# A graph layer with routed experts: the one-hot products of the tile stage read their weights as fp32, through a small copy

## The chip, the cores and the metric

One Trainium2 chip, one of its cores. The metric is the device time of one execution, in microseconds. The kernel before takes 3982.83 us, the median of three runs (3973.16 to 3984.31).

## What is computed

The reference, cut to what matters:

```python
def _L0_gnn_ref(x, W, bias, edge_row, edge_col, edge_val):   # x: layer-normalised, 12500 x 256
    h = x @ W
    msgs = h[edge_col] * edge_val[:, None]                   # 212500 edges
    agg = jax.ops.segment_sum(msgs, edge_row, num_segments=12500)
    return agg + bias

x = x + _L0_gnn_ref(_layernorm(x), W, bias, src, dst, edge_weight)
x = x + _L0_ffn_ref(_layernorm(x))      # 8 experts 256 -> 512 -> 256, the best two per row by a router
```

A row of `h` is fetched for every edge, weighted by `edge_weight` and added to the row of the node `src`. The expert part works on the result, row by row.

## The kernel before

The rows are cut into `NT` = 98 tiles of `P` = 128 nodes. The kernel has three parts.

**Preparation** (up to about 910 us). The edges are counted and sorted by node tile. The sorted list goes to DRAM as units. A unit is 128 partitions of `RUN` = 8 edges: 1024 edges, of which each has the row number of `h` to fetch, the node number and the weight as two fp16 halves, high and low. `h` is written to DRAM as `h_table`, each row as a high and a low fp16 half of 256.

**The tile stage** (about 910 to 3350 us), to which the change belongs. Tiles follow each other, and each engine has its own program, ordered by semaphores:

- SyncE, `serve` (lines 671 to 677): for each unit it waits until TensorE has used up the unit four before (`s_summed`), makes room for GpSimd (`s_room`) and loads a later unit of the list into the ring `listed` (`RL` = 8 slots).
- GpSimd, `gather` (lines 790 to 801): per unit eight indirect transfers (line 798), each of 128 rows of `h_table`, into the ring `stage` (`RU` = 4 units). It says that a unit is there (`s_gath`) in the middle of the next one.
- VectorE, `target_rows` (lines 1386 to 1407), once for each pair of a unit and a tile that the unit touches. This is called a pass here. Line 1392 subtracts the tile's first node number (`rel`). Line 1395 compares it with 0 to 127 (`equal`, one-hot rows of 8 x 128). Line 1403 multiplies the one-hot with the weights, once for the high halves and once for the low halves, each 128x1024, into the ring `target` (`TR` = 8 passes). There are 326 passes: a unit that lies across the border of two tiles has two.
- TensorE, `chunks` (lines 1821 to 1838): per pass eight times two matmuls, `target` by `stage` (lines 1832 and 1834), summed in PSUM. Line 1837 closes the tile.
- VectorE, `epilogue` (lines 1448 to 1464): from line 1458 on it adds the sum to `x`, normalises twice at once (lines 1426 to 1446) and writes `zb` (line 1446). TensorE turns `zb` (line 1851), ScalarE copies it, and the router's logits follow (lines 1856, 1858).
- Between these runs the dense expert work on half of the tiles: `hidden` (line 1885), ScalarE's GELU, the split into halves by VectorE (line 1510, an fp32 minus an fp16 operand), `expert` (line 1902) and the sums (line 1528). The rows of the other tiles are routed and handled in the last part.

What sets the order around the change is VectorE's own program, `step(t)`: the rest of tile t's passes (seldom any), the passes of tile t + 1 (`ahead`), then the epilogue of tile t, then the expert work and the choice of experts. TensorE's is `chunks(t)`, `hidden`, `transposes(t)` (which waits for `zb`), `expert`, `logits(t)`. So the passes of tile t + 1 stand on VectorE ahead of the epilogue of tile t.

**The routed part** (from about 3381 us). GpSimd scatters the routed rows by expert (line 815), TensorE works through blocks of 256 rows (lines 1954, 1970, 1987), and GpSimd gathers the results (line 830).

Of the kernel before, what the change touches and what calls it, by code (L numbers as in the profile page):

```python
# [5 lines left out]
def gnn_moe_layer_kernel(  # L6
# [42 lines left out]
    fp32 = mybir.dt.float32  # L49
# [6 lines left out]
    ds = bass.ds  # L56
    AX = mybir.AxisListType

    P = 128
    N, D = x.shape  # L60
    E = src.shape[0]
    NE, _, HID = W1.shape
    KD = D // P
    KH = HID // P
# [13 lines left out]
    RUN = 8  # L78
# [43 lines left out]
    with ctx:  # L122
        ctx.enter_context(nc.allow_non_contiguous_dma(reason="small constants, one element per row"))

        def sb(name, shape, dt):
            return ctx.enter_context(nc.sbuf_tensor(name, shape, dt))

        def sem(name):
            return ctx.enter_context(nc.semaphore(name))
# [88 lines left out]
        wfull = sb("wfull", [P, 2, SB, 32], fp32)  # L218
        wT = sb("wT", [P, P], fp32)
        rel = sb("rel", [P, RUN], fp16)  # L220


        UNIT = RUN * 2 * D
# [233 lines left out]
        s_gat = [sem(f"s_gat{k}") for k in range(RU)]  # L457
        s_gath = sem("s_gath")
        s_rel = sem("s_rel")
        s_eq = sem("s_eq")  # L460
        s_tgt = sem("s_tgt")
        s_summed = sem("s_summed")
# [59 lines left out]
        def reached(eng, s, value, gate=True):  # L522

            if isinstance(value, int):
                if value > 0:
                    eng.wait_ge(s, value)
                return
            eng.wait_ge(s, value)
            if gate:
                eng.sem_inc(s_gate, 1)  # L530
# [549 lines left out]
        def _(dve):  # L1080
# [305 lines left out]
            def target_rows(u, t):  # L1386
                i = u + t
                at = (u % RL) * WORDS
                listed_f = listed[:, :, :].rearrange("p u w -> p (u w)")
                listed_h = listed_f.bitcast(fp16)  # L1390
                reached(dve, s_list, 16 * (u + 1), gate=False)
                nc.vector.tensor_scalar(rel[:, :], listed_f[:, ds(at + RUN, RUN)], tile_no[:, ds(t, 1)], None,  # L1392
                                        ALU.subtract).then_inc(s_rel, 1)
                reached(dve, s_rel, i + 1, gate=False)
                nc.vector.tensor_tensor(  # L1395
                    equal[:, :, :, :], pair_no[:, :, :].unsqueeze(1).to_broadcast([P, RUN // 2, P, 2]),
                    rel[:, :].rearrange("p (j e) -> p j e", e=2).unsqueeze(2).to_broadcast([P, RUN // 2, P, 2]),
                    ALU.is_equal).then_inc(s_eq, 1)
                reached(dve, s_eq, i + 1, gate=False)
                reached(dve, s_summed, i + 1, gate=False)  # L1400
                for part in range(2):
                    two = listed_h[:, ds(2 * at + (4 + part) * RUN, RUN)].rearrange("p (j e) -> p j e", e=2)
                    made = nc.vector.tensor_tensor(  # L1403
                        target[:, ds((i % TR) * TGT + part * (TGT // 2), TGT // 2)].rearrange(
                            "p (j s e) -> p j s e", j=RUN // 2, e=2),
                        equal[:, :, :, :], two.unsqueeze(2).to_broadcast([P, RUN // 2, P, 2]), ALU.mult)
                made.then_inc(s_tgt, 1)

            def table(t, b, least, biggest):
                return dve.value_load(t[0:1, ds(b, 1)], min_val=least, max_val=biggest)  # L1410

            def ahead(t):
                first = table(lo_i, t, 0, NU)
                end = table(ahead_i, t, 1, NU + 1)
                with dve.Fori(first, end) as u:
                    target_rows(u, t)

            def rest(t):
                first = table(ahead_i, t, 1, NU + 1)
                end = table(end_i, t, 1, NU + 1)  # L1420
                with dve.If(first < end):
                    with dve.Fori(first, end) as u:
                        target_rows(u, t)
# [217 lines left out]
            nc.vector.memset(acc[:, 0, :, :].rearrange("p q d -> p (q d)"), 0.0)  # L1641
            nc.vector.memset(xTh[:, 0, :, :].rearrange("p k n -> p (k n)"), 0.0)
            nc.vector.memset(xTl[:, 0, :, :].rearrange("p k n -> p (k n)"), 0.0).then_inc(s_clear, 1)
            ahead(0)
            for t in range(NT + SB + 1):
                step(t)
# [62 lines left out]
        def _(pe):  # L1709
# [111 lines left out]
            def chunks(b):  # L1821
                reached(pe, s_x1, b, gate=False)
                nc.tensor.matmul(psA[:, :], one_h[:, :], bias_hl[:, :], start=True, stop=False)
                first = pe.value_load(lo_i[0:1, ds(b, 1)], min_val=0, max_val=NU)
                end = pe.value_load(end_i[0:1, ds(b, 1)], min_val=1, max_val=NU + 1)
                with pe.Fori(first, end) as u:
                    i = u + b
                    reached(pe, s_gath, u + 1, gate=False)
                    reached(pe, s_tgt, i + 1, gate=False)
                    for c in range(RUN):  # L1830
                        at, rows = (i % TR) * TGT + (c // 2) * (2 * P) + c % 2, (u % RU) * UNIT + c * (2 * D)
                        nc.tensor.matmul(psA[:, :], target[:, ds(at, P, 2)], stage[:, ds(rows, 2 * D)], start=False,  # L1832
                                         stop=False)
                        last = nc.tensor.matmul(psA[:, 0:D], target[:, ds(at + TGT // 2, P, 2)],  # L1834
                                                stage[:, ds(rows, D)], start=False, stop=False)
                    last.then_inc(s_summed, 1)
                nc.tensor.matmul(psA[:, 0:1], zero_h[:, 0:P], zero_h[:, 0:1], start=False,
                                 stop=True).then_inc(s_agg, 1)
# [88 lines left out]
            for t in range(NT + SB + 1):  # L1927
                i = t - SB
                if t < NT:
                    chunks(t)  # L1930
                if t - 1 in place_of:
                    ranks(t - 1)
                if 0 <= i < NEX and i % NE == 0:
                    weights_T(i // NE)
                if 0 <= i < NEX:
                    hidden(i)
                if t < NT:
                    transposes(t)
                if 1 <= i <= NEX:
                    expert(i - 1)  # L1940
                if 0 <= i < NEX and i % NE == 0:
                    b2_terms(i // NE)
                if t < NT:
                    logits(t)
# [50 lines left out]
            for n in range(NBL):  # L1995
                h, m = block_of(n)
                e = pe.value_load(expert_i[0:1, h, m:m + 1], min_val=0, max_val=NE - 1)
# [39 lines left out]
```

## Time and profile before

| | |
|---|---|
| median of three runs | 3982.83 us (3973.16 to 3984.31) |
| the profiled execution | 3981.84 us, of it the span of the profile 3979.7 us |
| mean granted TensorE clock | 0.919 of full speed |
| tile stage | first sum closed at 936.7 us, last at 3344.9 us |
| busy share PE, DVE, ACT, POOL | 80%, 61%, 33%, 64% |

PE is TensorE's matmul side, DVE is VectorE, ACT is ScalarE, POOL is GpSimd, SP is SyncE. All times count from the start of the span, in us. In a line of the timeline stand start, duration, engine, line of the kernel, operation and the tensors (out <- in); in square brackets stands how long the engine had been idle and what ended that. "x2" says that two like instructions are merged, and the duration is that of both together. In a group of instructions stand the shape and the count, then the busy time in us and the mean of one in ns, then the idle time before them. "issue" is time in which the engine waited for nothing that the profile shows.

### The profile page before, as it was taken

The numbers are of one execution on the slowest core, as the hardware profiler recorded it, in microseconds if no ns is written. First come the engines' busy times: TensorE is split into PE (matmuls) and PEld (weight loads), VectorE is DVE, ScalarE is ACT, GpSimd is POOL, SyncE is SP. The second block draws the span as 40 slices with busy tenths as digits, with TensorE's granted clock in tenths as the row PEclk, the third lists the DMA queues.
The fourth block names the chain that finished last, engine by engine and source line by source line (L and its number), as shares of the span: only waits on it lengthen the run. The fifth ranks groups of instructions, "written<-read, shape, count | busy, mean of one in ns | idle before, by whom it ended". The sixth has DMA issues, their size and how long they took to land.

```text
span 3979.7 us, 75949 instructions
## 1 busy us (share of the span) xinstructions
PE 3194.3 (80%) x20888; PEld 2076.7 (52%) x20888; DVE 2415.8 (61%) x6037; ACT 1331.0 (33%) x2857; POOL 2538.3 (64%) x2491
## 2 busy tenths in 40 slices
PE   6677767824788899898988998998988989099983
PEld 4444444412455555555555555555555556088862
DVE  9699334514666666666666666676666665144563
ACT  1354656720222222222222222222222222066651
POOL 1241457877777777777777777777777776630264
PEclk9899989966899999999999999999999999599996
DMA  4341110003434334434343434343334346552463
GB/s 154 106 117 60 33 36 15 8 12 92 117 110 119 110 113 114 119 112 120 112 117 110 117 110 120 109 115 108 114 111 120 108 118 104 175 165 86 125 202 113
DMA packets 288427, 420.20 MB, mean 106 GB/s; under 512 B 89733, under 2 KB 218314, under 8 KB 288138
## 3 DMA queue, kind: packets, MB, share of 16 engines
q0 software_dynamic: 109280, 279.33, 25.2%
q1 hardware_dynamic: 112536, 72.81, 6.4%
q10 hardware_dynamic: 66324, 64.42, 5.1%
q8 instruction: 157, 2.57, 0.3%
q14 instruction: 130, 1.06, 0.1%
HBM read 339.36 MB, written 76.98 MB: 105 GB/s over the span
## 4 chain that ended last, share of the span: by engine, by line
PE 36%; DVE 14%; issue 11%; POOL 7%; DVEq 5%; DMA 2%; ACT 1%; SPq 1%; ACTq 0%; POOLq 0%
PE twin L1902 7%; PE twin L1832 6%; PE bank L1902 6%; POOL area L798 5%; DVE area L1395 3%; PE twin L1834 3%; DVEq L1410 2%; DVE area L1403 2%; PE twin L1885 2%; PE bank L1885 2%; PE twin L1970 2%; PE twin L1987 2%; POOL zs L815 2%; PE bank L1970 1%; PE bank L1987 1%
## 5 line engine op out<-in xcount | busy, mean ns | idle before, releaser
L798 POOL DMA_INDIRECT area<-h_table,listed x1856 | 1864.3, 1004 | 606.0 <-issue 542.9
L1832 PE MATMUL twin<-area 128*128 x2608 | 880.9, 385 | 76.7 <-POOLq L797 38.3
L1834 PE MATMUL twin<-area 128*128 x2608 | 718.2, 275 | 0.0
L973 ACT ACTIVATE area<-twin,b_t 128x512 f32<-128x512 f32 x192 | 132.0, 687 | 1446.0 <-PE twin L1885 860.2
L1403 DVE TENSOR_TENSOR area<-area,listed 128x1024 f16 x652 | 422.6, 689 | 106.9 <-DVE area L1395 94.9
L1832 PEld LDWEIGHTS twin<-area 128*128 x2608 | 257.0, 99 | 415.2 <-issue 183.3
L766 POOL DMA_INDIRECT edge_list<-area,didx x256 | 313.0, 1223 | 77.1 <-issue 77.1
L1902 PE MATMUL twin<-w2h,area 128*128 128x256 f16 x1536 | 338.6, 317 | 0.0
L751 POOL TENSOR_TENSOR area<-area 128x256 f16<-128x256 f32 x98 | 80.9, 829 | 339.8 <-ACT area L862 339.6
L1834 PEld LDWEIGHTS twin<-area 128*128 x2608 | 257.1, 99 | 49.1 <-issue 0.2
L1902 PE MATMUL bank<-w2h,area 128*128 128x256 f16 x1536 | 267.7, 273 | 0.0
L1785 PE MATMUL twin<-area 128*128 128x512 f16 (+1 forms) x448 | 173.0, 392 | 113.7 <-ACT area L909 65.9
L1392 DVE TENSOR_SCALAR rel<-listed,tile_no 128x8 f16 x326 | 77.8, 239 | 297.9 <-issue 251.0
L1510 DVE TENSOR_TENSOR area<-area 128x512 f16<-128x512 f32 x384 | 244.0, 688 | 17.2 <-ACT area L975 17.2
L1902 PE MATMUL twin<-w2l,area 128*128 128x256 f16 x768 | 243.7, 317 | 0.0
L1395 DVE TENSOR_TENSOR area<-pair_no,rel 128x1024 f16<-128x1024 f16 x326 | 225.7, 692 | 11.2
L917 ACT ACTIVATE area<-twin 128x512 f16<-128x512 f32 (+1 forms) x448 | 228.9, 565 | 5.5 <-PE twin L1785 5.2
L1885 PE MATMUL twin<-area,w1h 128*128 128x512 f16 x768 | 229.5, 380 | 0.0
L1885 PE MATMUL bank<-area,w1h 128*128 128x512 f16 x768 | 228.8, 380 | 0.0
L1851 PE MATMUL bank<-ident,zb 128*128 128x128 f32 x196 | 44.9, 316 | 207.7 <-DVE zb L1446 207.4
L1671 DVE TENSOR_TENSOR area<-area 128x512 f16<-128x512 f32 x132 | 91.4, 692 | 197.8 <-ACT area L1045 197.8
L828 POOL DMA_DIRECT2D area<-out_dram x50 | 29.3, 586 | 285.5 <-issue 220.6
(339 smaller groups left out, 6505.3 us busy)
## 6 DMA issues: line engine op xcount, KB each, us to landing
area<-h_table,listed POOLq DMA_INDIRECT x1856
area<-in_x_dram SPq DMA_DIRECT2D x194, 128.0 KB, 2.2
area<-zs SPq DMA_DIRECT2D x66, 256.0 KB, 2.9
ys<-area ACTq DMA_DIRECT2D x66, 256.0 KB
out_dram<-area ACTq DMA_DIRECT2D x100, 128.0 KB, 2.6
h_table<-area SPq DMA_DIRECT2D x97, 128.0 KB, 1.7
xt<-in_x_dram ACTq DMA_DIRECT2D x97, 128.0 KB
area<-in_L_ffn_W_dram ACTq DMA_DIRECT2D x16, 512.0 KB, 4.0
```

The costliest lines, as they stand in the source:

```text
L766: pool.indirect_dma_start(out=list_v, out_offset=bass.IndirectOffsetOnAxis(ap=didx[B % 4][:, j, r:r + 1], axis=0), in_=record[:, B % 4, j, ...
L798: pool.indirect_dma_start(out=stage[:, (k % RU) * UNIT + 2 * D * c:(k % RU) * UNIT + 2 * D * (c + 1)], out_offset=None, in_=h_table[:, :], ...
L917: nc.scalar.activation(ohs[:, g % 2, PER * j:PER * j + w, :].rearrange("p c s -> p (c s)"), slot(n)[:, 0:w * P], ACT.Exp, scale=SHARP).the ...
L973: nc.scalar.activation(h32[:, m, :], psH[m][:, :], ACT.Gelu, scale=1.0 / WSCALE, bias=b1_t[:, e * KH + m:e * KH + m + 1])
L1395: nc.vector.tensor_tensor(equal[:, :, :, :], pair_no[:, :, :].unsqueeze(1).to_broadcast([P, RUN // 2, P, 2]), rel[:, :].rearrange("p (j e) ...
L1403: made = nc.vector.tensor_tensor(target[:, ds((i % TR) * TGT + part * (TGT // 2), TGT // 2)].rearrange("p (j s e) -> p j s e", j=RUN // 2, ...
L1510: nc.vector.tensor_tensor(hl[:, i % 2, m, :], h32[:, m, :], hh[:, i % 2, m, :], ALU.subtract).then_inc(s_hl, 1)
L1785: nc.tensor.matmul(slot(n)[:, 0:w * P], digits_T[:, g % 2, :], rh[:, PER * j:PER * j + w, :].rearrange("p c s -> p (c s)"), start=True, st ...
L1832: nc.tensor.matmul(psA[:, :], target[:, ds(at, P, 2)], stage[:, ds(rows, 2 * D)], start=False, stop=False)
L1834: last = nc.tensor.matmul(psA[:, 0:D], target[:, ds(at + TGT // 2, P, 2)], stage[:, ds(rows, D)], start=False, stop=False)
L1885: last = nc.tensor.matmul(psH[m][:, :], a, r, start=(k == 0 and n == 0), stop=(k == KD - 1 and n == 2))
L1902: last = nc.tensor.matmul(half_bank(q), a, r[:, e, m, :], start=(m == 0 and n == 0), stop=(m == KH - 1 and n == 2))
```

## The change

The weights of a pass, two times eight fp16 values per partition, are copied into a new fp32 tile `share`, and the two products of line 1403 read their weights from there. The one-hot operand and the result stay fp16. Before the copy overwrites `share` it waits until the products of the pass before are done (`s_tgt`); for that the semaphore starts at 1, and TensorE waits for one more.

```diff
@@ -218,6 +218,7 @@
         rel = sb("rel", [P, RUN], fp16)
+        share = sb("share", [P, 2, RUN], fp32)
@@ -457,6 +458,7 @@
         s_rel = sem("s_rel")
+        s_share = sem("s_share")
@@ -1391,15 +1393,19 @@
                 nc.vector.tensor_scalar(rel[:, :], listed_f[:, ds(at + RUN, RUN)], tile_no[:, ds(t, 1)], None,
                                         ALU.subtract).then_inc(s_rel, 1)
+                reached(dve, s_tgt, i + 1, gate=False)
+                nc.vector.tensor_copy(share[:, :, :].rearrange("p f c -> p (f c)"),
+                                      listed_h[:, ds(2 * at + 4 * RUN, 2 * RUN)]).then_inc(s_share, 1)
                 reached(dve, s_rel, i + 1, gate=False)
                 nc.vector.tensor_tensor(
                     equal[:, :, :, :], pair_no[:, :, :].unsqueeze(1).to_broadcast([P, RUN // 2, P, 2]),
                     rel[:, :].rearrange("p (j e) -> p j e", e=2).unsqueeze(2).to_broadcast([P, RUN // 2, P, 2]),
                     ALU.is_equal).then_inc(s_eq, 1)
+                reached(dve, s_share, i + 1, gate=False)
                 reached(dve, s_eq, i + 1, gate=False)
                 reached(dve, s_summed, i + 1, gate=False)
                 for part in range(2):
-                    two = listed_h[:, ds(2 * at + (4 + part) * RUN, RUN)].rearrange("p (j e) -> p j e", e=2)
+                    two = share[:, part, :].rearrange("p (j e) -> p j e", e=2)
                     made = nc.vector.tensor_tensor(
...
@@ -1641,6 +1647,7 @@
+            dve.sem_inc(s_tgt, 1)
             ahead(0)
@@ -1826,7 +1833,7 @@
-                    reached(pe, s_tgt, i + 1, gate=False)
+                    reached(pe, s_tgt, i + 2, gate=False)
```

## Rows read from the trace of the kernel before

**Rows 1.** The page: busy shares, the chain that ended last, the group of line 1832.

```profile
PE 3194.3 (80%) x20888; PEld 2076.7 (52%) x20888; DVE 2415.8 (61%) x6037; ACT 1331.0 (33%) x2857; POOL 2538.3 (64%) x2491
...
PE 36%; DVE 14%; issue 11%; POOL 7%; DVEq 5%; DMA 2%; ACT 1%; SPq 1%; ACTq 0%; POOLq 0%
...
L1832 PE MATMUL twin<-area 128*128 x2608 | 880.9, 385 | 76.7 <-POOLq L797 38.3
```

**Rows 2.** Line 1837 alone: ns min/median/max, first and last start.

```profile
L1837 PE MATMUL twin<-zero_h x98: 172/172/173, 936.7 to 3344.9; 1*128 1x1 f16 x98
```

**Rows 3.** PE's waits, 1300 to 3300: us in total, times, longest.

```profile
PE bank L1851 <- DVE zb L1446: 166.7, 54, 5.7
...
PE twin L1832 <- POOLq L797: 0.3, 1, 0.3
```

**Rows 4.** Timeline of DVE in one tile (four passes, then the epilogue).

```profile
2092.43 0.23 DVE L1392 TENSOR_SCALAR rel<-listed,tile_no 128x8 f16 x1 [3.25 <-issue]
...
2097.49 0.23 DVE L1392 TENSOR_SCALAR rel<-listed,tile_no 128x8 f16 x1
2097.75 0.69 DVE L1395 TENSOR_TENSOR area<-pair_no,rel 128x1024 f16<-128x1024 f16 x1
2098.77 1.29 DVE L1403 TENSOR_TENSOR area<-area,listed 128x1024 f16 x2 [0.33 <-DVE area L1395]
2099.98 0.22 DVE L1392 TENSOR_SCALAR rel<-listed,tile_no 128x8 f16 x1
...
2102.54 0.41 DVE L1458 TENSOR_TENSOR area<-xt,twin 128x256 f32<-128x256 f32 x1
...
2105.90 0.41 DVE L1446 TENSOR_SCALAR zb<-area,mv,rs 128x256 f32<-128x256 f32 x1
```

**Rows 5.** Timeline of PE in the same tile.

```profile
2101.55 0.38 PE L1885 MATMUL bank<-area,w1l 128*128 128x512 f16 x1
2106.46 0.41 PE L1851 MATMUL bank<-ident,zb 128*128 128x128 f32 x2 [4.53 <-DVE zb L1446]
```

**Rows 6.** Timeline of DVE and PE in the next tile.

```profile
2130.40 0.41 DVE L1446 TENSOR_SCALAR zb<-area,mv,rs 128x256 f32<-128x256 f32 x1
...
2131.91 0.38 PE L1851 MATMUL bank<-ident,zb 128*128 128x128 f32 x2
```

**Rows 7.** Groups of DVE by shape, whole span: line 1403.

```profile
L1403 DVE TENSOR_TENSOR area<-area,listed 128x1024 f16 x652 | 422.6, 689 | 106.9 <-DVE area L1395 94.9 <-PE twin L1834 12.0
```

**Rows 8.** The same view: subtractions of fp16 from fp32, and a small operation.

```profile
L1510 DVE TENSOR_TENSOR area<-area 128x512 f16<-128x512 f32 x384 | 244.0, 688 | 17.2 <-ACT area L975 17.2
...
L1469 DVE TENSOR_TENSOR area<-xT,area 128x256 f16<-128x256 f32 x48 | 20.0, 416 | 9.5 <-ACT area L962 9.5
...
L1542 DVE TENSOR_TENSOR eqr<-iota,ixrf 128x16 f32<-128x16 f32 x50 | 8.8, 176 | 1.7
...
L1659 DVE TENSOR_TENSOR area<-area 1x2048 f16<-1x2048 f32 x1 | 2.3, 2281 | 0.0
```

**Rows 9.** The chain, 2000 to 2120, and busy times of 2101.7 to 2111.5.

```profile
2081.49 2.62 PE twin L1902 x24
...
2106.87 4.29 PE twin L1902 x24
...
2101.70:2111.50 9.80, 5.27 (x33) 3.94 (x32) 7.37 (x25) 2.31 (x5) 7.56 (x8) 0.83 0.50 143
```

The last of these rows has the window and its length, then the busy time and count of PE, PEld, DVE, ACT and POOL, then the granted clock, the DMA share and GB/s.

**Rows 10.** Timeline of POOL at the end of the stage.

```profile
3372.56 0.95 POOL L798 DMA_INDIRECT area<-h_table,listed  x1 [0.30 <-issue]
3381.39 1.00 POOL L815 DMA_INDIRECT zs<-area,slot_i  x1 [7.88 <-DMA area<-h_table,listed]
```

**Rows 11.** Line 798: group of 1300 to 3300, all durations, one gather.

```profile
L798 POOL DMA_INDIRECT area<-h_table,listed x1506 | 1513.2, 1005 | 488.8 <-issue 441.1 <-SPq L675 39.2 <-DMA listed<-edge_list 5.2
...
L798 POOL DMA_INDIRECT area<-h_table,listed x1856: 947/953/1492, 907.9 to 3372.6; - x186
...
2003.42 1.45 POOL L798 DMA_INDIRECT area<-h_table,listed  x1 [0.31 <-issue]
```

## The prediction, made before the changed kernel was run

> **What bounds the kernel now.** I read the page first [rows 1]: VectorE (DVE) is busy 61% of the span, TensorE (PE) 80%, GpSimd (POOL) 64%. No engine is full, so the averages decide nothing. The chain of waits is shared by PE (36%), DVE (14%) and time at issue (11%). The change lies in one stage only, the loop over 98 node tiles. By its last matmul of each tile it paces at (3344.9 - 936.7) / 97 = 24.83 us per tile [rows 2].
>
> Next, who waits for whom in that stage. Between 1300 and 3300 us, some 80 tiles, PE waits 166.7 us in 54 waits for zb, the normalised tile that DVE's line 1446 writes [rows 3]. It waits 0.3 us for gathers, and the products of line 1403, which the change edits, are no large waits of their own. What PE lacks is not the products but what DVE does behind them.
>
> The timeline of one tile shows why [rows 4]. DVE runs the passes for the next tile's units (compare, two products) first, and only then the epilogue of this tile. In the tile shown it makes four passes from 2092.43, the epilogue starts at 2102.54, right behind the last product, and zb is finished at 2106.31. PE had finished its own work at 2101.93 and stood still until 2106.46 [rows 5]. In this tile every microsecond in a pass is a microsecond of the tile. The other kind: in the next tile PE had four iterations and DVE three passes; zb was finished at 2130.81 and PE came to it at 2131.91 without a wait [rows 6]. There DVE has about 1.1 us to spare.
>
> The 652 products of line 1403 [rows 7] are two a pass, so 326 passes over 98 tiles, 3.33 per tile, so one tile in three has a fourth pass. Of the 80 tiles 26 do not wait (32 of 98). The 54 waits average 3.1 us; where the pass count of DVE is four they are 4 to 4.5, as here, so the rest are near 2: about a third of the tiles each.
>
> **The price of one pass.** A pass now takes 2.49 us from one line 1392 to the next (2097.49 to 2099.98, [rows 4]).
>
> The products. The instruction of 128x1024 with all operands fp16 takes 0.689 us [rows 7]. After the change one operand is fp32. The rows nearest to that are the mixed subtractions, fp32 minus fp16 into fp16: 0.416 us for 256 elements, 0.688 for 512, and 2.281 for 2048 on one partition [rows 8]. 512 mixed elements cost what 1024 of fp16 do. Between the last two an element costs (2281 - 688) / 1536 = 1.037 ns, so 1024 take 0.688 + 0.531 = 1.22 us. The other pair gives 1.063 ns and 1.23 us. What these rows do not show is the operand that repeats eight values, so the lower bound is no change, 0.69 us; the upper is 1.23. I take 1.22: +0.53 for each of two, +1.06 a pass.
>
> The copy of 16 elements is new. The nearest row is an operation of 128x16 at 0.176 us [rows 8]. It stands between line 1392 and the comparison, where 0.03 us was free. Its wait for s_tgt asks for the last product of the pass before, which ends 0.08 us after line 1392 starts (2098.77 + 1.29 against 2099.98); behind it in DVE's queue stand the copy and the comparison. Two things pull the price apart: the address of the copy may be worked out only after that wait, and the 0.33 us between comparison and product [rows 4] may get shorter, since the products no longer work out an address in listed. Bounds: -0.10 us (the gap shrinks and the copy hides) to +0.33 (0.18 of copy and 0.15 of address work). I take +0.11, the middle. The later wait for s_share is on something long finished: nothing. The other edits, the pre-increment and PE's wait for i + 2, only shift a count by one: nothing. So a pass grows by 1.17 us, with ends at 0.96 and 1.39 as long as the product slows.
>
> **The sum, against the profiled execution (3981.84 us; the median of the three runs is 3982.83, 1 us away).**
> - 321 passes (all but the first tile's five, which lie under the first gathers) by 1.17: +376.
> - The 32 tiles in which DVE was early give 1.1 us of cover each: -35.
> - The first tiles wait for gathers: 38.3 us of PE's idle time at line 1832 are put to POOL over the whole span [rows 1] and 0.3 in the window of [rows 3]. POOL runs on meanwhile; I count half as given back: -18.
> - TensorE's clock. After the wait of 4.53 us the first 24 products of line 1902 took 4.29 us, against 2.62 in the tile before, where the wait was short [rows 9]; the granted clock of that stretch was 0.83, so part of it was at 1.2 GHz and not 2.4. That is 1.67 us. The third of tiles that now waits about 2 us will wait about 5.5 and pays it: 32 by 1.67 = +53. The third with no wait will wait about 2.4, between the two cases; half of them: +27. The last third pays already.
> - The end of the stage. Now POOL's last gather starts at 3372.56, 28 us after PE's last sum, and the scatter that the next stage waits for starts at 3381.39 [rows 10]. With slower tiles POOL is a full ring of four units ahead and ends soon after PE. The scatter then moves up by 15 to 20 us relative to the stage: -18.
>
> Sum: 376 - 35 - 18 + 53 + 27 - 18 = +385, so 3981.84 + 385 = 4367 us. The stage would go from 24.8 to about 28.9 us per tile. DVE's new busy time (652 by 0.53, and 326 copies) is +400 us, so almost none of it is hidden.
>
> What late DVE leaves others waiting for: PE for zb; ACT behind PE; the ring of targets (eight deep) stays ahead, for the passes of a tile are still made a tile early.
>
> **GpSimd.** A gather takes 0.953 us and 0.30 between, mean 1.005 [rows 11]: 1856 / 98 = 18.9 per tile by 1.305 is 24.7 us, as long as a tile now. It waits for room 39 us in 2000 [rows 11], so it is nearly the bound itself. At 28.9 us per tile it has 4 us to spare. But gathers get longer under DVE's two-input operations: 1.45 us at 2003.42 [rows 11], while DVE ran four of the mixed subtractions. The trace puts all such lengthening at 0.05 us on the mean gather, 1 us per tile; products 1.8 times as long make that 1.5 to 2, within the slack, so nothing is added.
>
> The Trainium skill (SBUF — State Buffer, Who interferes with whom) speaks more strongly against the change: a Vector instruction with two SBUF inputs locks out a GpSimd instruction that reads SBUF until it ends. By that rule each gather that meets a product would wait some 0.6 us on average, about 6 per tile, and POOL would need 28 us: still just under the tile, and the sum would stand. The trace agrees on the direction alone; its median gather is 0.953 us.
>
> **The rivals.**
> - Not slower: the product keeps its rate. The mechanism lies in line 1403: if the repeated fp32 operand costs no reading of its own, the product stays at 0.69 us, the copy fills the gap and one address less is worked out. Then a pass changes by -0.10 to +0.33 us; near zero the time is 3980, at the far end 4090. It decides at a product under 0.72 us. Against it: every mixed row runs at the slow rate. 0.04, most of it no change.
> - Hidden: GpSimd paces the stage, and DVE's time disappears under 24.7 us per tile. For it: the gathers fill the stage. Against it: PE waits 166.7 us for zb and 0.3 for gathers, and a tile cannot end before its DVE passes do. 3985 us. 0.02.
> - The clock goes further down. Waits of 5.5 to 9 us may cost twice 1.67 us in every tile: 97 by 1.67 = +160, 4527 us. For it: the longest waits now are 5.7 us [rows 3], so nothing longer is shown. 0.09.
> - GpSimd becomes the bound after all. If every gather that meets a product waits the whole of it (6 by 1.2), POOL needs 24.7 + 7.2 = 32 us per tile: (32 - 24.8) by 97 = +700, 4680 us. Against it: the median gather. 0.04.
> - The forecast: 0.81.
>
> **How the numbers follow.** The likeliest case gives 4367. Its bounds: a pass at +0.96 gives 308 in place of 376, and no clock loss takes off another 53 to 80, but hardly both: 4270. A pass at +1.39 gives +70, and with some more clock loss 4490, which takes in a part of the third rival. About 0.2 is left out. About 0.3% (12 us) is what a measurement of this kernel can tell from no change. Faster 0.01, same 0.04, slower 0.95.
>
> **What would show it.** In the profile after: line 1403 at 1.22 us x652 (under 0.72: the first rival); 3.6 to 3.7 us from one line 1392 to the next; PE's waits for zb at 5 to 6 us on the mean and in nearly every tile; 24 products at 4.3 us in most tiles, and a granted clock near 0.9 in the stage; GpSimd waiting for room 3 to 4 us per tile where it now waits half a microsecond; the last gather close behind PE's last sum; the stages before and after unchanged. The prediction is wrong if a pass grows by 1.2 us and the tile by much less (something hides it), or if PE waits for gathers at line 1832.

## The result, and the profile after

The changed kernel takes 4363.06 us, the median of four runs (4358.88 to 4364.65), against 3983.57 us for the kernel before beside it. The ratio is 1.0957, with a 95% interval of 1.0937 to 1.0977: 380 us slower. The forecast was 4367 us, 1.096 of the kernel before.

The page of the changed kernel (a line of the kernel has a number higher by 2 to 7 than before: 1392 is now 1394, 1403 is 1409, 1446 is 1452, 1832 is 1839, 1851 is 1858, 1902 is 1909, 798 is 800):

```profile
span 4359.8 us, 76276 instructions
PE 3263.3 (75%) x20888; PEld 2110.6 (48%) x20888; DVE 2786.0 (64%) x6363; ACT 1333.9 (31%) x2857; POOL 2717.3 (62%) x2491
```

DVE's busy time is up by 370 us (400 were forecast), and its share only from 61% to 64%, since the span grew as much. A reader of shares alone would not see that DVE's work sets the pace.

Its groups by shape, whole span, against [rows 7] and the 128x16 of [rows 8]:

```profile
L1409 DVE TENSOR_TENSOR area<-area,share 128x1024 f16 x652 | 776.9, 1232 | 97.9 <-issue 83.3 <-DVE area L1400 9.2 <-PE twin L1841 5.4
...
L1397 DVE CAST share<-listed 128x16 f32 x326 | 59.2, 181 | 5.6 <-issue 0.4
```

The product went from 0.689 to 1.232 us, the rate of the mixed subtractions. The copy takes 0.181 us.

The end of one pass, two whole passes and what follows them in the timeline of DVE, against [rows 4]:

```profile
2191.80 1.21 DVE L1409 TENSOR_TENSOR area<-area,share 128x1024 f16 x1
2192.93 0.22 DVE L1394 TENSOR_SCALAR rel<-listed,tile_no 128x8 f16 x1
2193.18 0.17 DVE L1397 CAST share<-listed 128x16 f32 x1
2193.26 0.69 DVE L1400 TENSOR_TENSOR area<-pair_no,rel 128x1024 f16<-128x1024 f16 x1
2194.23 2.43 DVE L1409 TENSOR_TENSOR area<-area,share 128x1024 f16 x2 [0.29 <-issue]
2196.58 0.28 DVE L1394 TENSOR_SCALAR rel<-listed,tile_no 128x8 f16 x1
...
2200.24 0.41 DVE L1464 TENSOR_TENSOR area<-xt,twin 128x256 f32<-128x256 f32 x1
```

The copy starts at 2193.18, 0.17 us behind the end of the products that it waits for (2193.01) and 0.03 behind the end of line 1394. The comparison starts 0.08 us after the copy and runs beside it, so the copy adds next to nothing. The gap ahead of the products is 0.29 us and was 0.33. The epilogue (line 1464) still starts right behind the last product. Over all pairs of passes within a tile (229 of them, from the starts of line 1392 and 1394 in the two traces) the mean distance went from 2.528 to 3.632 us: +1.104.

Who waits for whom, 1300 to 3700 us, against [rows 3] and [rows 11]; PE's waits first, then POOL's:

```profile
PE bank L1858 <- DVE zb L1452: 445.3, 83, 9.7
...
PE twin L1839 <- DVE area L1409: 0.3, 1, 0.3
```

```profile
POOL area L800 <- SPq L677: 224.5, 52, 10.2
```

83 tiles fit into this window at 28.8 us each, and there are 83 waits: every tile waits now, 5.4 us on the mean where 54 of 80 waited 3.1. The products themselves are waited for once. Gathers are not in the list of PE's waits at all. GpSimd waits for room 224.5 us in these 2400; it was 39.2 in 2000. The gathers moved from nearly the bound to 2.7 us of slack a tile, although they became longer (see GpSimd below).

The end of the stage (source line 1844, then POOL's timeline), against [rows 2] and [rows 10]:

```profile
L1844 PE MATMUL twin<-zero_h x98: 172/172/173, 937.6 to 3732.3; 1*128 1x1 f16 x98
```

```profile
3753.13 1.34 POOL L800 DMA_INDIRECT area<-h_table,listed  x1 [0.30 <-issue]
3762.44 1.27 POOL L817 DMA_INDIRECT zs<-area,slot_i  x1 [7.98 <-DMA area<-h_table,listed]
```

A tile takes (3732.3 - 937.6) / 97 = 28.81 us, 3.98 more: +386 us over the stage. The scatter starts 30.1 us behind the last sum and started 36.5 us behind it: the end gives 6 us back.

### The profile page after: what moved, and what is told of

Same layout as the page of the kernel before. It is cut to its first block and busy times, and to the rows that moved or that the text cites. A ratio compares the mean times of both kernels' runs of the same rounds, so it can differ in the third digit from the quotient of the medians.

```text
span 4359.8 us, 76276 instructions
## 1 busy us (share of the span) xinstructions
PE 3263.3 (75%) x20888; PEld 2110.6 (48%) x20888; DVE 2786.0 (64%) x6363; ACT 1333.9 (31%) x2857; POOL 2717.3 (62%) x2491
## 5 line engine op out<-in xcount | busy, mean ns | idle before, releaser
L800 POOL DMA_INDIRECT area<-h_table,listed x1856 | 2045.2, 1102 | 808.5 <-issue 543.7
L1409 DVE TENSOR_TENSOR area<-area,share 128x1024 f16 x652 | 776.9, 1232 | 97.9 <-issue 83.3
L1858 PE MATMUL bank<-ident,zb 128*128 128x128 f32 x196 | 58.1, 395 | 525.3 <-DVE zb L1452 525.3
L1909 PE MATMUL twin<-w2h,area 128*128 128x256 f16 x1536 | 396.3, 353 | 0.0
L1858 PEld LDWEIGHTS bank<-ident,zb 128*128 128x128 f32 x196 | 26.1, 186 | 568.6 <-issue 564.2
L1909 PE MATMUL twin<-w2l,area 128*128 128x256 f16 x768 | 271.3, 353 | 0.0
L960 ACT ACTIVATE xT<-bank,bet,gam 128x128 f32<-128x128 f32 x196 | 79.2, 454 | 627.9 <-PE bank L1858 627.9
L1516 DVE TENSOR_TENSOR area<-area 128x512 f16<-128x512 f32 x384 | 241.6, 690 | 4.1 <-ACT area L977 4.1
L1909 PEld LDWEIGHTS twin<-w2h,area 128*128 128x128 f16 x1536 | 197.6, 129 | 59.1
```

Of the source, the lines that this page charges most:

```text
L800: pool.indirect_dma_start(out=stage[:, (k % RU) * UNIT + 2 * D * c:(k % RU) * UNIT + 2 * D * (c + 1)], out_offset=None, in_=h_table[:, :], ...
L1409: made = nc.vector.tensor_tensor(target[:, ds((i % TR) * TGT + part * (TGT // 2), TGT // 2)].rearrange("p (j s e) -> p j s e", j=RUN // 2, ...
L1516: nc.vector.tensor_tensor(hl[:, i % 2, m, :], h32[:, m, :], hh[:, i % 2, m, :], ALU.subtract).then_inc(s_hl, 1)
L1909: last = nc.tensor.matmul(half_bank(q), a, r[:, e, m, :], start=(m == 0 and n == 0), stop=(m == KH - 1 and n == 2))
```

## The experiments

Theory: the operand's type halves the rate of the products; they stand on VectorE ahead of the epilogue, so the time goes to TensorE's wait for zb in full, and the longer wait costs clock on top. Against it stood: the copy and its waits as the cost; a threshold; the sum of VectorE's work or the gathers as the bound and not the order; a longer part of the tile behind zb that has other causes than the clock. The ratios below are to the kernel before, run beside the experiment.

**The copy alone.**

```diff
-        share = sb("share", [P, 2, RUN], fp32)
+        share = sb("share", [P, 2, RUN], fp16)
```

> The changed kernel with the new tile share as fp16: copy, waits and semaphores stay, the products are all fp16 again. Theory (the operand type slows the product): product back at 0.69 us, a pass 2.57 us (3.65 less 2 by 0.54), so +0.08 us on the pass of before; 321 passes make +26 us and a few us of clock: 4010 us. Rival (the copy and its wait in the middle of VectorE's queue are the cost): a pass stays above 3.2 us and the time above 4200 us.

Measured: 3984.91 us, ratio 1.0017 (1.0007 to 1.0028). The mean distance of two passes is 2.548 us, +0.020.

```profile
L1409 DVE TENSOR_TENSOR area<-area,share 128x1024 f16 x652 | 422.1, 689 | 98.0 <-issue 88.0 <-DVE area L1400 6.9 <-PE twin L1841 3.1
...
L1397 DVE COPY share<-listed 128x16 f16 x326 | 57.9, 178 | 7.1 <-issue 0.4
```

The copy, its wait for the products of the pass before and the counts shifted by one cost 7 us together (3 to 11 by the interval). The 4010 us that were expected counted 0.08 us a pass, four times what it was. 326 copies of 0.178 us are 58 us of busy time, of which hardly any shows. The type of the operand is the rest: about 373 of the 380 us.

**One product of the two.**

```diff
-                    two = share[:, part, :].rearrange("p (j e) -> p j e", e=2)
+                    two = (share[:, 0, :] if part == 0 else listed_h[:, ds(2 * at + 5 * RUN, RUN)]).rearrange("p (j e) -> p j e", e=2)
```

> Only the first of the two products reads its weights from share as fp32, the second reads fp16 from the list as before. Theory: the product means 0.69 and 1.23 us, a pass is 3.1 us (+0.63), 321 passes +202, cover -35 and -18, clock of the third of tiles that now waits about 3.9 us +53, end of stage -6: +196, 4178 us. Rival (a threshold: the extra time is first hidden and then breaks through, or one slow product is as bad as two): below 4080 or above 4300 us.

Measured: 4161.11 us, ratio 1.0464 (1.0444 to 1.0484). In the groups by shape the two products stand side by side:

```profile
L1409 DVE TENSOR_TENSOR area<-area,share 128x1024 f16 x326 | 399.7, 1226 | 95.9 <-DVE area L1400 51.1 <-issue 30.7 <-PE twin L1841 14.0
L1409 DVE TENSOR_TENSOR area<-area,listed 128x1024 f16 x326 | 223.8, 687 | 0.0
```

Here one-hot and result are the same for both products, and only the weights' type differs. The distance of two passes is 3.080 us, +0.552, half of the full change; the time is 46 thousandths up, close to half of 96. Nothing here looks like a threshold. PE's waits for zb (1300 to 3500) are 290.2 us in 74.

**The passes behind the epilogue, in the changed kernel.**

```diff
-                if t + 1 < NT:
-                    ahead(t + 1)
                 if t - 1 in place_of:
                     ranks(t - 1)
                 if t < NT:
                     epilogue(t)
...
+                if t + 1 < NT:
+                    ahead(t + 1)
                 if 0 <= i < NEX:
                     h_low(i)
```

> The changed kernel with the passes of tile t+1 moved behind the epilogue of tile t on VectorE; the work is the same. Theory (the passes cost because they stand ahead of zb): TensorE's waits for zb fall to near nothing and VectorE runs without long waits; its busy time of about 20.5 us per tile with 3 us of issue and some gaps gives 26 to 27 us per tile where 29 is now, so 4130 to 4180 us. Rival (VectorE's sum of work or the gathers set the tile, not the order): within 30 us of 4360.

Measured: 4170.13 us, ratio 1.0484 (1.0466 to 1.0503), 193 us less than the changed kernel with the same work. PE's waits, 1300 to 3500:

```profile
PE twin L1839 <- POOLq L799: 117.4, 35, 8.4
PE twin L1927 <- DVE area L1534: 94.6, 10, 13.6
PE bank L1874 <- DVE cum L1555: 65.5, 28, 2.4
PE twin L1839 <- DVE area L1409: 37.1, 42, 5.2
PE bank L1858 <- DVE zb L1452: 25.5, 24, 2.1
```

The waits for zb are nearly gone, as the order says. Others came in their place: for gathers, for the expert sums of line 1534 that now stand behind the passes, and for the products. So half of the loss was the place of the passes in VectorE's queue.

The other half is not settled. It was expected to be VectorE's longer work, but the largest wait is now for gathers, and GpSimd is nearly full. Its gathers in this kernel, 1300 to 3300:

```profile
L800 POOL DMA_INDIRECT area<-h_table,listed x1398 | 1530.1, 1095 | 470.5 <-issue 417.9 <-SPq L677 46.5 <-DMA area<-h_table,listed 4.0
```

It waits for room only 46.5 us in 2000. A tile takes 26.8 us here and 24.6 in the kernel before with the same order (below), and a gather 1.095 us on the mean and 0.985 there: 18.9 gathers by 0.11 are 2.1 of the 2.2 us between them. So the longer gathers, which the products cause (see GpSimd below), explain the rest as well as VectorE's own work does. No run separates the two.

**Idle matmuls in the wait, first try.** To see what the clock costs, TensorE works through matmuls that nobody reads.

```diff
+                for _ in range(FILL[t]):
+                    nc.tensor.matmul(psT, ones_h[:, :], w1h[:, 0, 0, 0:2 * P], start=True, stop=True)
                 pe.wait_ge(s_z, t + 1)
```

> The changed kernel with idle matmuls of 128x256 into the unused PSUM area ahead of TensorE's wait for zb, 8 to 84 a tile, to fill 0.5 us less than the wait that the trace shows in that tile (the first six tiles get none). Theory (part of the loss is TensorE's clock): the granted clock of the stage goes to 1.0, 24 products take 2.6 us after every wait, the tail of a tile behind zb falls by 1.7 us where it was slow, in all 110 to 150 us: 4215 to 4250 us. Rival (the longer tail comes from the work of ScalarE or VectorE behind zb, and the clock costs nothing): 4360 us or more.

Measured: 4343.05 us, ratio 1.0915 (1.0894 to 1.0936), only 20 us less than the changed kernel, between theory and rival. The granted clock of the whole rose from 0.886 to 0.934. The waits of PE say what went wrong:

```profile
PE bank L1858 <- DVE rank L1561: 100.4, 29, 6.1
```

In a tile behind a routed one TensorE waits for `ranks` first, which VectorE does behind the passes. The fill stood behind that wait and made zb's matmul late: on the mean of 90 tiles it came 22.1 us after the tile's start, not 20.7. So this run cannot say what the clock costs.

**Idle matmuls in the wait, second try**, ahead of both waits and in another PSUM bank:

```diff
                 reached(pe, s_xTh, t)
+                if FILL[t]:
+                    pe.wait_ge(s_yadd, SB * (quad(t - SB - 1) - 1) + 2)
+                for _ in range(FILL[t]):
+                    nc.tensor.matmul(psY[0][:, 0:2 * P], ones_h[:, :], w1h[:, 0, 0, 0:2 * P], start=True, stop=True)
                 reached(pe, s_read, len([r for r in routed if r < t]))
```

> As the filled kernel of before, but the idle matmuls stand ahead of TensorE's wait for the ranks as well, in a PSUM bank that is free by then, so that they lie inside the wait and do not lengthen it. The trace of the changed kernel has, per tile, 1.64 us more behind zb than the fastest tiles; the first filled kernel took that to 0.04 but moved zb's matmul back by 1.4 us. Theory (that excess is TensorE's clock): 90 tiles by 1.5 us = -135 us, 4225 us, zb's matmul at the same distance from the tile's start as in the changed kernel (20.7 us). Rival (the fill only moves the time): within 25 us of 4343.

Measured: 4222.46 us, ratio 1.0611 (1.0594 to 1.0628): 141 us less than the changed kernel. zb's matmul comes 20.8 us after the tile's start, as in the changed kernel, and the part of the tile behind it went from 8.29 to 6.71 us on the mean of 90 tiles: 142 us, the whole gain. The groups of PE show the matmuls that follow the wait (the first half of an expert, "twin") and the second half ("bank"). In the kernel before, 1300 to 3300:

```profile
L1902 PE MATMUL twin<-w2h,area 128*128 128x256 f16 x1280 | 286.8, 320 | 0.0
L1902 PE MATMUL bank<-w2h,area 128*128 128x256 f16 x1280 | 223.1, 273 | 0.0
```

In the changed kernel, 1300 to 3700, and the window's busy times (the granted clock is the third number from the end):

```profile
L1909 PE MATMUL twin<-w2h,area 128*128 128x256 f16 x1328 | 347.9, 356 | 0.0
...
L1909 PE MATMUL bank<-w2h,area 128*128 128x256 f16 x1328 | 231.8, 273 | 0.0
```

```profile
1300.00:3700.00 2400.00, 1919.02 (x11395) 1187.00 (x11394) 1683.84 (x4123) 546.15 (x960) 1712.54 (x1552) 0.90 0.34 98
```

The same with the waits filled, 1300 to 3300:

```profile
L1914 PE MATMUL twin<-w2h,area 128*128 128x256 f16 x1152 | 201.7, 274 | 0.0
L1914 PE MATMUL bank<-w2h,area 128*128 128x256 f16 x1152 | 200.4, 273 | 0.0
```

```profile
1300.00:3300.00 2000.00, 1919.00 (x13180) 1290.92 (x13178) 1483.35 (x3617) 480.26 (x845) 1497.05 (x1365) 1.00 0.37 103
```

A matmul of the first half has a mean of 356 ns in the changed kernel, 320 in the kernel before and 274 with the waits filled, where the granted clock is 1.00 (2.4 GHz throughout) and not 0.90. The second half is 273 in all three, so in the unfilled kernels too it runs at the full clock. So 141 of the changed kernel's microseconds are time at 1.2 GHz behind a wait. The kernel before has a part of that too.

**The same two remedies in the kernel before.** The order, by the edit shown for the changed kernel:

> The kernel before with the passes of tile t+1 moved behind the epilogue of tile t. Theory: TensorE's waits for zb (2 us per tile) go, VectorE has 22 us of work in a tile, and then the gathers set the pace: 18.9 by 1.305 = 24.7 us per tile where 25.0 is now (waits in the first tiles included), so 3950 to 3975 us, and TensorE waits for gathers at line 1832. Rival (the order is worth what the waits for zb show, and the gathers have room): 25.0 less 2.0 and 0.9 of clock, 22.1 us per tile, 3700 us. A third way: with passes just in time TensorE waits for them instead: 4000 us or more.

Measured: 3958.36 us, ratio 0.9948 (0.9934 to 0.9962). And the filled waits, with counts from the trace of the kernel before:

> The kernel before with idle matmuls in TensorE's waits for zb (0 to 46 a tile, 0.6 us less than each wait). Theory (the clock is worth 0.86 us per tile there too, but the gathers allow only 24.7 us per tile): 3950 to 3965 us. Rival (the gathers do not limit): 90 by 0.8 = -72 us, 3910 us.

Measured: 3957.07 us, ratio 0.9940 (0.9926 to 0.9954). They are 21 and 23 us faster than the kernel before, about half a percent, and the intervals leave out no change. The waits, 1300 to 3300: PE and then POOL in the reordered kernel, the same in the filled one.

```profile
PE twin L1832 <- POOLq L797: 110.9, 22, 7.3
```

```profile
L798 POOL DMA_INDIRECT area<-h_table,listed x1520 | 1496.8, 985 | 504.9 <-issue 452.4 <-SPq L675 49.2 <-DMA area<-h_table,listed 2.1
```

```profile
PE twin L1833 <- POOLq L798: 48.9, 29, 4.5
```

```profile
L799 POOL DMA_INDIRECT area<-h_table,listed x1525 | 1532.3, 1005 | 469.8 <-issue 451.0 <-SPq L676 7.5 <-DMA area<-h_table,listed 7.3
```

TensorE now waits for gathers (0.3 us before). Both kernels close a tile each 24.6 us. In the filled kernel that is what 18.9 gathers take: GpSimd waits for room 7.5 us in 2000, so the gathers fill the stage. In the reordered one the gathers are shorter (985 ns), and GpSimd still waits 49.2 us for room while TensorE waits 110.9 for gathers; which of the two limits it, the time of the gathers or a ring of four units, is not shown.

The two fills compare as follows. In the changed kernel 1.58 of the 8.29 us behind zb's matmul went away and nothing came in their place. In the kernel before 0.81 of 7.52 us went away, 73 us over 90 tiles, but zb's matmul came 17.90 us after the tile's start and not 17.37, which took 47 of them back. So the fill gave 141 us where the gathers had slack, and 23 of some 73 where they had none.

## Why the prediction was right

**The product.** +0.53 us each from the mixed subtractions; measured +0.543. The repeating operand of eight values, the point that no row showed, made no difference. The rival in which the product keeps its rate is out.

**The copy.** This term was mis-sized: +0.11 us a pass as the middle of -0.10 and +0.33, measured +0.020 in the copy alone. The 0.17 us between the end of the products and the copy are there (whether they are the address work that was forecast, the trace does not say), but all but 0.03 us of them lie beside line 1394. The comparison runs beside the copy, and the gap ahead of the products shrank by 0.04. A pass grew by 1.104 us and not 1.17: 354 us over 321 passes where 376 were summed.

**The cover.** -35 us of slack in early tiles: 3.34 passes by 1.104 are 3.69 us per tile, and zb's matmul moved by 3.37 (tiles 6 to 95, from the traces, 17.37 to 20.74 us after the tile's start). The difference is 0.32 us per tile, 29 us; that it is cover in early tiles is the reading of the forecast and was not tried by itself.

**The clock.** +80 us; the part of a tile behind zb's matmul, above that of the fastest tiles, went from 0.86 to 1.64 us per tile, +70 us over these 90 tiles. The filled kernel, in which this excess is 0.05 us, shows that it is clock. The rival with twice the loss is out. By the length of the wait, from the two traces (the tiles that close a set of experts left out), the excess is 0.0 us for waits under 1 us, 0.3 to 0.6 for 1 to 3 us (single tiles show either 0.0 or about 1.7), 2.0 to 2.2 for 3 to 6.5 us, and 1.9 for longer ones, up to 9.7 us: it does not grow further. The single price of 1.67 us was a little low. What the sum did not say is how much of it is at stake in all: 141 us.

**The first tiles.** -18 us: the stage grew by 386 us; the 90 tiles hold 3.37 + 0.78 = 4.15 us each, 373 us, and the other seven 13 us, where their 20 passes by 1.104 us would give 22. So some 9 us were hidden there; that it was under waits for gathers is the reading of the forecast.

**The end of the stage.** -18 us, measured -6. The step that failed is "ends soon after PE". The last gather started 20.8 us behind PE's last sum (27.7 before). The last two units need the room of units that the last tile still sums, and that tile's passes end at 3726.8, 3729.4 and 3732.4; the units started at 3728.20 and 3740.11, so sixteen gathers and a wait of 4.53 us for landings lay behind that however early GpSimd was. The direction was right, the size a third.

**GpSimd.** The forecast was 1.5 to 2 us of longer gathers per tile. It was 18.9 by (1.102 - 0.953) = 2.8:

```profile
L800 POOL DMA_INDIRECT area<-h_table,listed x1856: 947/954/2015, 905.6 to 3753.1; - x186
```

The longest gather went from 1.492 to 2.015 us and the median stayed at 0.954. Two gathers of the timeline of POOL, around the products of line 1409 at 2191.80 and 2194.23 that are shown above:

```profile
2191.88 1.96 POOL L800 DMA_INDIRECT area<-h_table,listed  x1 [0.30 <-issue]
2194.14 0.95 POOL L800 DMA_INDIRECT area<-h_table,listed  x1 [0.30 <-issue]
```

The first starts 0.08 us into a product and takes 1.01 us more than the median; that product ends at 2193.01. The second is under way when the next product starts, and is not delayed. The whole trace is like that. In the changed kernel 410 of the 1856 gathers take over 1 us. Each of them starts while a VectorE instruction with both inputs in SBUF runs: 262 a product, 32 a comparison (line 1400), 116 a mixed subtraction (lines 1516 and 1475). Each is longer by what that instruction still had to run, less 0.12 to 0.13 us. Turned round, of the 267 gathers that start over 0.04 us into a product with more than 0.17 us of it left, 257 are longer; of the 112 that start closer behind its start, only five. Of the 105 gathers that were first, with a product starting beside them, none is longer, and neither is any of the 124 that start beside a VectorE instruction with an input in PSUM alone. In the kernel before, all 276 gathers over 1 us fit the same way, 107 of them on a product of 0.69 us.

The Trainium skill's rule (SBUF — State Buffer, Who interferes with whom) fits these: two SBUF inputs, the whole rest of the instruction, and whoever is first holds the other up. What was wrong in the 4.6 us that the forecast worked out by it (1.0 as now and 3.6 more) is that every gather that meets a product would be delayed; those that are first are not, and 2.8 us were measured. Either way it stayed inside the slack of this kernel: GpSimd waited for room 2.7 us per tile, where 3 to 4 were forecast. But it is not free: 18.9 gathers now need 18.9 by (1.102 + 0.30) = 26.5 us, where they needed 24.7, so with gathers of this length no order of VectorE's work brings this kernel back to the old time per tile.

So the terms missed by -22 (pass), +6 (cover), -10 (clock), +9 (first tiles) and +12 us (end), together -5; the profiled executions differ by 380 where 385 were forecast. The errors partly cancel: the closeness of 4363 to 4367 is in part luck, and a sum right to 20 us would have been as good an argument. What carried it was the step from a pass to a tile: each wait for zb ends with VectorE's last pass and epilogue.

## What to carry to other kernels

Look at what stands in the queue behind an operation, not at who reads its result. Here nobody waited for the products, and their extra time was paid almost in full, because an epilogue stood behind them; moving them behind it gave half of it back. One fp32 operand was enough to slow this two-operand VectorE instruction from 0.69 to 1.23 us, and a small copy between two dependent instructions cost 0.02 us. Before speeding up what waits, look at how full the next engine is: filling the waits gave 141 us with slack on GpSimd and 23 us without. And look at whom a longer instruction holds up on other engines: here it lengthened the gathers by 1.8 us per tile, which did not show in this order and is close to the limit in a better one.

## What was not expected of the hardware

TensorE's clock behind waits of 2 to 10 us was worth more than thought: filling the waits with matmuls that nobody reads, up to 83 a tile, took 3.2% off the changed kernel and 0.6% off the kernel before. The copy of 0.18 us with a wait of its own cost 0.02 us a pass. And gathers issued by GpSimd became longer only when they started while a VectorE instruction with both inputs in SBUF was already running (410 of 410), up to 2.0 us and not 0.95; a gather that was first was never delayed by a product (0 of 105). Nothing was run in which the gathers are kept away from the products.
